# A decoder block's second layer: the queries of groups 1 to 3 copied from SBUF to SBUF into their stack, without a DRAM tensor between

## The reference

```python
def _L1_xattn_ref(queries, keys, values, Wq, Wk, Wv, Wo):
    B, S, D, H = (2, 512, 256, 16)
    HD = D // H
    q = split_heads(queries @ Wq.T)
    k = split_heads(keys @ Wk.T)
    v = split_heads(values @ Wv.T)
    scores = jnp.einsum('bhqd,bhkd->bhqk', q, k) * scale
    attn = jax.nn.softmax(scores, axis=-1)
    ctx = jnp.einsum('bhqk,bhkd->bhqd', attn, v)
    ...
x = x + _L0_xattn_ref(_layernorm(x, axis=-1), ctx_1024, ctx_1024, ...)
x = x + _L0_ffn_ref(_layernorm(x, axis=-1), ...)
x = x + _L1_xattn_ref(_layernorm(x, axis=-1), ctx_1024, ctx_1024, ...)
x = x + _L1_ffn_ref(_layernorm(x, axis=-1), ...)
```

## Time and profile before

| | us |
|---|---|
| median of 3 runs | 1032.26 |
| lowest and highest of them | 1027.65, 1036.03 |
| the profiled execution | 1021.1 |
| its span, first to last instruction | 1019.6 |

### The profile page before, as it was taken

One profiled execution on the slowest core, in us unless ns is written; L12 is line 12 of the kernel. 1 busy time (PEld: TensorE's weight loads), 2 busy tenths in 40 slices (PEclk: granted clock), 3 DMA queues, 4 the chain that ended last, 5 costly groups with the idle time before them and its releaser, 6 DMA issues. The chain is left out here.

```text
span 1019.6 us, 14969 instructions
## 1 busy us (share of the span) xinstructions
PE 834.2 (82%) x5166; PEld 541.5 (53%) x5167; DVE 467.8 (46%) x1091; ACT 271.9 (27%) x545; POOL 243.1 (24%) x304
## 2 busy tenths in 40 slices
PE   6858998899897998975769999955776878878985
PEld 4634666557564545543436555544344546546663
DVE  2526473356446451331124433422854846857732
ACT  1212211411321210211112222211233533534551
POOL 4533413404004340110001111135230242111011
PEclk8979999999998799997779999987586979999997
DMA  7867424323308473566555455365357577575410
GB/s 209 227 221 234 124 80 151 98 90 113 108 1 275 174 228 104 165 168 176 134 133 144 146 161 149 122 192 125 92 121 123 126 155 129 122 139 112 99 36 19
DMA packets 78366, 140.81 MB, mean 138 GB/s; under 512 B 16626, under 2 KB 57331, under 8 KB 76291
## 3 DMA queue, kind: packets, MB, share of 16 engines
q1 hardware_dynamic: 64212, 93.07, 30.8%
q10 hardware_dynamic: 6158, 26.44, 13.0%
q0 software_dynamic: 7936, 20.52, 8.0%
HBM read 108.24 MB, written 30.20 MB: 136 GB/s over the span
## 5 line engine op out<-in xcount | busy, mean ns | idle before, releaser
L1226 PE MATMUL ps<-rw,rowsT 128*128 x288 | 140.8, 634 | 2.7 <-ACT rowsT L1186 0.6
L1560 DVE TENSOR_REDUCE mxh<-ps 112x2 f32<-112x750 f32 x128 | 115.3, 932 | 57.0 <-PE ps L1843 42.9
L1725 ACT ACTIVATE d_pT<-ps 125x448 f32<-125x448 f32 x192 | 90.5, 548 | 87.7 <-PE ps L1863 67.8
L1843 PE MATMUL ps<-kst,qst 96*112 96x375 bf16 x256 | 74.8, 387 | 40.3 <-DVE mxh L1560 21.4
L921 PE MATMUL ps<-x1T,sw 128*128 128x448 f32 x256 | 102.6, 547 | 6.2 <-DVE gluT L441 4.3
L1226 PEld LDWEIGHTS ps<-rw,rowsT 128*128 128x128 f32 x288 | 55.2, 202 | 66.9 <-issue 66.9
L1152 DVE TENSOR_TENSOR h<-ps,rb 128x512 f32<-128x512 f32 x36 | 24.9, 692 | 124.0 <-PE ps L1226 124.0
L921 PEld LDWEIGHTS ps<-x1T,sw 128*128 128x128 f32 x256 | 46.8, 190 | 51.6 <-issue 39.4
L1131 POOL DMA_DIRECT2D yscr<-y x36 | 19.7, 547 | 228.4 <-DVE y L1165 228.4
L1241 PE MATMUL ps<-rw,gT 128*128 x288 | 68.1, 379 | 0.8 <-ACT gT L1190 0.8
L1241 PEld LDWEIGHTS ps<-rw,gT 128*128 128x128 f32 x288 | 54.6, 190 | 23.3 <-issue 17.8
(11 more groups left out here) (226 smaller groups left out, 1235.0 us busy)
## 6 DMA issues: line engine op xcount, KB each, us to landing
rb<-in_rb SPq DMA_DIRECT2D x36, 512.0 KB, 4.1
rw<-in_rw SPq DMA_DIRECT2D x24, 512.0 KB
kscr<-ka SPq DMA_DIRECT2D x16, 567.0 KB
kst<-kscr ACTq DMA_DIRECT2D x12, 567.0 KB, 6.2
ctxT<-in_ctx_t SPq DMA_DIRECT2D x16, 378.0 KB
cT<-in_ctx_t SPq DMA_DIRECT2D x16, 378.0 KB, 8.1
ctxn<-in_ctx SPq DMA_DIRECT2D x16, 375.0 KB
vt<-vscr ACTq DMA_DIRECT2D x14, 398.4 KB
```

What stands on the lines that cost most here:

```text
L1226: last = mm(bank[1 + 2 * q + k], rowsT[:, q, c * P:(c + 1) * P], w[:, e, c, :], start=c == 0, stop=c == C - 1)
L1560: V.tensor_reduce(mxh[:, 2 * g:2 * g + 2], ps[0:S, 2 * (g % 2):2 * (g % 2) + 2, 0:K], axis=AX_X, op=ALU.max).then_inc(s["s_max"], 1)
L1725: A(pT[:, q % 2, k, :], bank[4 + k][0:KC, 0:QUAD * S], ACT.Exp).then_inc(s["p_ready"], 1)
L1843: last = mm(bank[2 * (g % 2) + k][0:S, 0:K], qst[0:DEPTH, i % 2, h, j * S:(j + 1) * S], kst[0:DEPTH, b % 4, h, 0:K], start=True, stop=True)
```

## The change

The DRAM tensor `qscr`, the semaphore `q_out` and the function `store_queries` are gone. `load_queries` now waits for GpSimd's last part (`q3_ready`) and issues six copies from `qa` straight into `qst`. It stands where the store stood, ahead of `exps(b, 1)`. The two waits on `q_out` that kept `qa` from being overwritten (ScalarE in `queries`, GpSimd in `split_queries`) now wait for the copies of the group before.

```diff
         def split_queries(i):
             pool.wait_ge(s["q_read"], queries_counted(i))
             if i > 1:
-                pool.wait_ge(s["q_out"], (i - 1) * 16)
+                pool.wait_ge(*queries_in((i - 1) * G))
...
                 elif m == 0:
-
-                    a.wait_ge(s["q_out"], (i - 1) * 16)
+                    a.wait_ge(*queries_in((i - 1) * G))
...
-        def store_queries(i):
+        def load_queries(i):
+
             a.wait_ge(s["q3_ready"], G + i)
-            a.dma_start(qscr[i].rearrange("s p x -> p s x"), qa[:].rearrange("p s c t -> p s (c t)")).then_inc(s["q_out"], 16)
-
-        def load_queries(i):
-            a.wait_ge(s["q_out"], i * 16)
             for r, k in enumerate((0, 0, 0, 1, 1, 2)):
-                a.dma_start(qst[r * HD:(r + 1) * HD, i % 2, :, :].rearrange("p h t -> p (h t)"),
-                            qscr[i, k].rearrange("(d g) x -> d (g x)", d=HD)).then_inc(s[f"qs_in{i % 2}"], 16)
+                a.dma_start(qst[r * HD:(r + 1) * HD, i % 2, :, :], qa[:, k, :, :]).then_inc(s[f"qs_in{i % 2}"], 16)
...
             if b % G == 1 and b // G + 1 < NG:
-                store_queries(b // G + 1)
+                load_queries(b // G + 1)
             exps(b, 1)
             exps(b, 2)
-            if b % G == 1 and b // G + 1 < NG:
-                load_queries(b // G + 1)
             if what is not None:
                 turned_over(what, i)
```

More of the change, by code:

```diff
@@ L1273, in second_layer @@
     QUAD = 4
-    yscr, kscr, vscr, qscr = (dram[n] for n in ("yscr", "kscr", "vscr", "qscr"))
+    yscr, kscr, vscr = (dram[n] for n in ("yscr", "kscr", "vscr"))
     ((wv1, cT, qst, vt, va, yg, xh, xhT, qa, qr, pT, outT, heads, res, mxh, mr, mparts, mT, rec),
@@ L1279, in second_layer @@
         "weights_in", "wf_ps", "wf_ready", "identb_ready", "below_in", "scaled", "added", "mixed", "xh_ready",
-        "q_ps", "q1_ready", "q_read", "q2_ready", "q3_ready", "q_out", "qs_in0", "qs_in1",
+        "q_ps", "q1_ready", "q_read", "q2_ready", "q3_ready", "qs_in0", "qs_in1",
         "k_in0", "k_in1", "k_in2", "k_in3", "v_in0", "v_in1", "s_ps", "s_max", "m_ready", "mT_ps", "mT_ready",
@@ L2027, in build_program @@
                 ("xg", [ROWS, D], F32), ("yscr", [NTILE * P, D], F32), ("kscr", [B, 3, P, C * KP], BF16),
-                ("vscr", [B, KC, NKC * NH * (HD + 1)], F32), ("qscr", [NG, 3, P, C * GS], BF16)):
+                ("vscr", [B, KC, NKC * NH * (HD + 1)], F32)):
             dram[name] = nc.dram_tensor(name, shape, dt, kind="Internal").ap()
```

## The result

Over 20 runs of each kernel the median went from 1029.68 to 1034.05 us; the ratio is 1.0055, with a 95% interval of 1.0033 to 1.0077. The change makes the kernel about half a per cent slower, where 1.2% faster was forecast. But the profiled execution of before was quicker than nearly all of its 20 runs (1020.07 to 1036.03), so the two profiles show more than the medians do.

The account below looks back on a forecast made before the run. PE bounds the kernel, and attention loses time where PE waits, partly for queries. -9.56 - 3.36 + 0.5 = -12.4 us, from 1032.3 to 1019.9 us, 1.2% faster; the forecast's own range was 1015 to 1025, the wide one 1008 to 1035.

Parts of the forecast that it names:

- What bounds the kernel: PE's three unnamed waits at the start of blocks 2, 6 and 10 are for the queries, 9.56 us in all.
- The chain after: The six copies, issued at the store's place, bring the queries 15 us after first issue, before PE needs them.
- The bound from above: Copies at the store's pace take 23.4 us in block 1, 15.4 in block 9; gain falls by 5.8 us.
- In time by 0.7 us: Block 10: the third group's queries come at 912.2, PE needs them at 912.9.
- Nothing stands behind these waits: Blocks 2, 6, 10 and block 9: no other wait replaces those removed, together 12.9 us.
- Removed waiting in block 9: PE's wait for the turned rows, through ScalarE's wait for the store's landing, goes: 3.36 us, a loss occurring once.
- The moved issues: ScalarE's six issues, 2.67 us, ahead of quarter 1's exponentials cost 0.5 us over three blocks; bounds 0 and 10.9.
- The clock: After block 2's stall PE's clock was lower; a shorter stall could return up to a microsecond, counted as 0.
- Late or uncovered: Rival, 20%: copies slower than the loads, or ScalarE's issues show; gain falls by 4 to 9 us, 1024 to 1029.
- The stalls go too: Rival, 10%: the two stalls in blocks 1 and 5 vanish with the store, another 10.85 us, 1009.
- the stalls grow: Rival, 12%: more in flight lengthens stalls of blocks 1 and 5, perhaps 9, by 10 to 16 us; 1030 to 1036.
- ScalarE is held by its queue: Rival, 8%: the copies' issues hold ScalarE, quarter 1's exponentials come 8.7 us late in each block; 1039 us.

Follow-up runs that it names:

- f3: Changed kernel with the values' load cut into 112 and 13 rows and GpSimd's eight gathers issued ahead of the queries' split; 996.1 us, ratio 0.9759 to before.
- e4: Changed kernel with the six copies issued where the loads stood, behind quarter 2's exponentials; 1020.1 us in a single execution.
- e5: Changed kernel with the values' load of blocks 1, 5 and 9 issued behind the six copies; 1029.5 us, ratio 1.0071 to before.
- e10: Changed kernel with only 5 of 125 values' rows loaded in blocks 1, 5 and 9 (results not the kernel's); 1012.1 us, ratio 0.9893 to before.
- e6: Changed kernel with every values' load cut into 112 and 13 rows; 1005.9 us, ratio 0.9850 to before.
- first pair: The first profiles of the kernels before and after, spans 1019.6 and 1031.8 us.
- second pair: The profiles of before_again and after_again, both kernels repeated unchanged on one chip, spans 1020.0 and 1038.2 us.
- before_again: The kernel before, unchanged, profiled once more on another chip; 1021.6 us in a single execution.
- f5: f3 with the six copies issued behind quarter 1's exponentials instead of ahead of them; 1003.4 us, ratio 0.9776 to before.
- after_again: The changed kernel, unchanged, timed and profiled once more beside the variants; 1038.1 us, ratio 1.0168 to before.
- e1: Kernel before with DRAM scratch rows padded, so its loads move in pieces of 1792 bytes instead of 14,336; 1026.5 us in a single execution.
- e3: Changed kernel with copies reading long runs of old queries from the stack's other slot (results not the kernel's); 1017.4 us in a single execution.
- e8: Changed kernel with the six copies issued by SP, behind the next block's rows of maxima, instead of ScalarE; 1036.4 us, ratio 1.0145 to before.

## Why the prediction was wrong, point by point

**What bounds the kernel.** Right. The three unnamed waits are waits for the queries: in f3, where the copies land 12.8 to 14.1 us after their issue, they are gone but for 0.5 us.

**The chain after: the failed step.** "I take the load's own time, 12.6 to 13.1 us, since their target is unchanged, and add 2 us because the values' load and, in two groups, the gathers are in flight beside them." The first half held: 13.1 to 14.3 us with neither the values nor the gathers in the way (f3, and group 3 of e4, e5 and e10), 14.0 to 16.4 with the gathers. The term of 2 us was mis-sized; it measured 13.4, 12.2 and 10.8 us (26.0, 24.8 and 23.9 against 12.6, 12.6 and 13.1). The values' load isn't something beside them that takes a share of a common rate. It is 398 KB on five engines, and each later transfer has five sixteenths of its pieces behind it. The gathers are the smaller part. Group 3 has none and is 10.8 us late all the same, 0.9 to 2.1 us faster than the others. Beside a load that is out of the way they cost 0.8 to 3.1 us (e5 and e10, groups 1 and 2 against 3), beside the cut one 4 to 5 (e6, last piece at 17.7 and 18.2 us, against f3, 12.8 and 14.1).

**The bound from above.** It was 23.4 us for block 1 and 15.4 for block 9, from the store's landing. The first was short by 2.6 us, the second by 8.5; for block 5 it was short by 1.4. (A slip beside it: queries at 778.7 that are needed at 773.7 lose 4.9 us, not 4.7.) Doubling the store's time assumed that it moves at one pace. It doesn't: eleven sixteenths of it went in 2 us and the rest waited for the values' load. In block 9, "had landed within 7.7 us" was taken as a sign of an open road; from 897.8 to 902.8 the values' load was on the five engines, and the 1792-byte pieces of the store, 74 ns each, write to DRAM, while into 16 partitions they take 170 to 260 ns.

**In time by 0.7 us.** With 15 us the third group's queries would have come just in time. This was said, and that the whole gain hung on the landing was the right reading of the risk.

**Nothing stands behind these waits.** Wrong at the start of block 10. The rows of maxima are three small copies from SP into the same stack, issued at 905.74 and needed at 917.6, and they came 14.9 us after issue (PE released at 920.63). Their pieces on the same engines were started from 911.5 to 917.2 only, between those of the copies. The prediction named the queues that the change moves past and not the engines under them. It cost 3.3 us in the first pair and 12.3 in the second, there at the start of block 2 above all (7.13 us). In e6 it is gone (0.9 us).

**Removed waiting in block 9.** Right: the 3.36 us at the turned rows are gone from after's waits, as are 7.8 us of the same kind in the second pair. That this loss occurs once was true only beside the stalls: before_again has it in block 5 too.

**The moved issues.** The six took 4.04, 4.94 and 3.85 us, not 2.67: it was SP's row that foretold them, not ScalarE's own loads. With the exponentials 3.7 to 4.8 us late, PE waited 1.30 us in block 5 and 0.21 in block 9, some 1.5 us where 0.5 was taken and 10.9 was the bound. Most of the cover held, and in f5 no gain is seen from moving them.

**The clock.** Counted at 0 as a possible gain, it was a loss of 3.0 us of matmul time in the first pair, with longer waits (7.44 and 5.93 us in place of 5.83 and 1.71) in front of the matmuls that then ran at a lower granted clock (0.50 from 926 to 930 us; before, 0.62 from 918 to 922 and 0.95 from 922 to 926). In the second pair PE's busy time differs by 0.4 us only, so the loss isn't a fixed part of the change. The window that the prediction reads for the stall of block 2 lies in block 1, behind the stall on the maxima; behind block 2's the clock is 0.50 as well (779 to 783). Here is a stretch of after_again ahead of its last wait, in windows (the last three columns: granted clock, DMA share, GB/s):

```profile
925.00:929.00 4.00, 0.81 (x12) 0.61 (x12) 0.00 (x0) 1.42 (x3) 0.00 (x0) 0.80 1.03 119
929.00:933.00 4.00, 0.00 (x0) 0.00 (x0) 0.00 (x0) 0.00 (x0) 0.00 (x0) 0.50 0.53 69
```

In the second window no engine computes, the DMA engines are half busy in sum and move 69 GB/s. The pieces in it are 58 of the copies (0.10 MB), which PE waits for, and 13 of the keys' load (0.16 MB), which it doesn't. The clock is at the lower of its levels (0.50, 1.2 GHz) by then.

**The base.** Carrying over the 11 us between the profiled execution and the median was right in size: the 20 runs have a median of 1029.7, 8.6 above that execution.

**The rivals.** *Late or uncovered* was right in kind: the copies are slower than the loads. But it gave as the reason that they are cut into eight times as many pieces, which e1 prices at 1.3 us at most, and its loss of 4 to 9 us of the gain stopped short of what happened, since it took the store's time as the worst. *The stalls go too* and *the stalls grow*: neither; they stayed as they were in the first pair (5.94 and 5.77 us). The price of the first, another 10.85 us, was wrong too: before_again lacks the stalls and is no faster. The time that came out, 1034.05, lies in the range that *the stalls grow* gave (1030 to 1036) and so just inside the wide range up to 1035; that is luck, since the stalls did not grow. *ScalarE is held by its queue*: slower, as it said, but by another mechanism. In after no issue took more than 1.66 us and a set at most 4.94; ScalarE was never held by 8.7 us. Only e3's copies of long runs held it for 7.5 to 7.9.

## What to carry to other kernels

Before moving a transfer to an earlier place, list what is in flight there and how many DMA engines each of those transfers uses, for a large one with 125 rows sat on five of them and held that share of everything issued behind it. Another queue was no way out: there the copies met the keys' load, which had stood behind them before. A transfer that moves eleven sixteenths of its pieces at once, pauses and then moves the other five is the sign, and it is readable in the trace of before; so are the five moves of the load's semaphore. When a wait is removed, ask also what it kept apart: here it kept the loads off the values' load, and only with that load cut into 112 and 13 rows did the shorter way pay.

## What the runs showed of the hardware that was not expected

- 125 rows of 3264 bytes used five of the sixteen engines; as 112 + 13 rows they were all started within 2 us in f3, and over 10 us on the five when the copies ran beside them (904.1 to 914.2).
- Six transfers of 224 KB, each into 16 partitions, took 12.6 to 14.3 us in all with the way clear, whether from DRAM or from SBUF, in pieces of 14,336 or of 1792 bytes (before, e1, f3, and e4's block 9): some 96 to 109 GB/s. A piece of 1792 bytes took 74 ns towards DRAM and 170 to 260 ns into 16 partitions.
- Three copies of a few KB on SP's queue took 14.9 us beside a large set on ScalarE's.
- On SP's queue the copies, with 640 of 768 pieces moved, stood still for 3 us while a load from ScalarE's queue, issued 3 us behind their first, was moved (e8, block 9).
- An issue of 128 pieces took 0.62 us in after's block 9 set (3.85 us for six), one of 16 rows about 0.45 (2.67 for six), and the store's single issue with 384 pieces 0.39. A count of pieces alone doesn't explain that.
